# An attention layer on one core: three turns of the probabilities moved ahead of two chunks of the output projection

## The reference

```python
xn = layernorm(x)                                  # x: (4, 512, 1024)
q, k, v = xn @ Wq.T, xn @ Wk.T, xn @ Wv.T          # 32 query heads, 8 key/value heads, 128 wide
q, k = rmsnorm(q) * q_norm_w, rmsnorm(k) * k_norm_w
scores = q @ k.T / sqrt(128) + alibi_bias          # causal
out = softmax(scores) @ v
s = concat_heads(out) @ Wo.T
g = silu(xn @ W.T + bias + lora(xn))
y = x + s * g
```

## Time and profile before

| what | value |
|---|---|
| median of 3 runs | 2855.52 us (2854.84 to 2856.85) |
| the profiled execution: its own time | 2851.0 us |
| the profiled execution: its span, first to last instruction | 2849.2 us |
| PE busy | 2763.9 us, 97% of the span |
| DVE, ACT, POOL busy | 2198.6 us (77%), 1259.9 us (44%), 1136.4 us (40%) |
| mean granted TensorE clock | 0.990 of full speed |

### The profile page before, as it was taken

How to read it: one execution, slowest core, us unless ns; L and a number is a source line. 1 busy time by engine, 2 the same in 40 slices (tenths; PEclk the granted TensorE clock), 3 DMA queues, 4 the chain that set the end, 5 groups by cost and what they waited for, 6 DMA issues and landing times.

```text
span 2849.2 us, 47788 instructions
## 1 busy us (share of the span) xinstructions
PE 2763.9 (97%) x18256; PEld 2516.4 (88%) x18256; DVE 2198.6 (77%) x5317; ACT 1259.9 (44%) x2907; POOL 1136.4 (40%) x555
## 2 busy tenths in 40 slices
PE   7999999998999999999899999999989999999997
PEld 6899999997889999999688999999878999999985
DVE  6877777778787777777878777777787877777788
ACT  3444444444344444444434444444443444444443
POOL 3334334333434434334353334443344433344334
PEclk9999999999999999999999999999999999999999
DMA  7222222212422221221341222222224222222213
GB/s 256 97 79 67 65 70 64 64 61 96 168 66 86 75 67 60 68 75 57 106 168 52 72 75 75 67 69 65 71 96 160 67 61 66 75 75 68 74 62 113
DMA packets 80659, 240.40 MB, mean 84 GB/s; under 512 B 9008, under 2 KB 17328, under 8 KB 79920
## 3 DMA queue, kind: packets, MB, share of 16 engines
q1 hardware_dynamic: 80432, 237.35, 25.2%
HBM read 217.39 MB, written 19.92 MB: 83 GB/s over the span
## 4 chain that ended last, share of the span: by engine, by line
PE 83%; DVE 14%; issue 2%; ACT 0%; DMA 0%; SPq 0%; POOL 0%; POOLq 0%; DVEq 0%; ACTq 0%
PE proj L402 20%; PE proj L403 20%; PE proj L404 20%; PE tr L472 4%; PE sc L402 3%; PE ot L403 3%; PE ot L404 3%; PE sc L404 3%; PE sc L403 3%; DVE g_buf L1155 3%; PE ot L402 3%; PE tr L484 2%; DVE sq L1060 2%; DVE prob L1126 1%; DVE xtok L1050 1%
## 5 line engine op out<-in xcount | busy, mean ns | idle before, releaser
L916 POOL TENSOR_TENSOR wb_lo<-stage_b,wb_hi 128x1024 fp32r<-128x1024 f32 x158 | 382.3, 2419 | 1424.6 <-ACT wb_hi L684 1424.6
L402 PE MATMUL proj<-wa_hi,xn_hi 128*128 128x256 f32 x3072 | 878.3, 286 | 0.9 <-issue 0.9
L404 PE MATMUL proj<-wa_hi,xn_lo 128*128 128x256 f32 x3072 | 869.3, 283 | 0.0
L403 PE MATMUL proj<-wa_lo,xn_hi 128*128 128x256 f32 x3072 | 869.2, 283 | 0.0
L402 PEld LDWEIGHTS proj<-wa_hi,xn_hi 128*128 128x128 f32 x3072 | 589.0, 192 | 2.5 <-issue 2.1
L403 PEld LDWEIGHTS proj<-wa_lo,xn_hi 128*128 128x128 f32 x3072 | 589.3, 192 | 0.3
L404 PEld LDWEIGHTS proj<-wa_hi,xn_lo 128*128 128x128 f32 x3072 | 588.9, 192 | 0.0
L911 POOL TENSOR_TENSOR wa_lo<-stage_a,wa_hi 128x1024 fp32r<-128x1024 f32 x192 | 463.1, 2433 | 228.7 <-ACT wa_hi L670 228.7
L709 ACT ACTIVATE prob<-prob,negmax 128x128 f32<-128x128 f32 (+3 forms) x512 | 286.5, 560 | 431.0 <-DVE negmax L1116 430.1
L402 PE MATMUL proj<-o_hi,wb_hi 128*128 128x512 f32 x1024 | 431.5, 421 | 41.7 <-DVE acc L1143 40.3
L1143 DVE TENSOR_TENSOR acc<-acc,proj 128x512 f32<-128x512 f32 x480 | 326.9, 682 | 116.0 <-PE proj L404 113.3
(11 more groups left out here) (120 smaller groups left out, 4778.9 us busy)
## 6 DMA issues: line engine op xcount, KB each, us to landing
stage_a<-wa SPq DMA_DIRECT2D x196, 512.0 KB, 3.6
stage_b<-wo SPq DMA_DIRECT2D x128, 512.0 KB, 3.7
stage_b<-weff SPq DMA_DIRECT2D x30, 512.0 KB, 3.8
xtok<-x_tok SPq DMA_DIRECT2D x4, 2048.0 KB, 8.6
outT<-acc SPq DMA_DIRECT2D x32, 256.0 KB, 2.0
gate_dram<-x_buf SPq DMA_DIRECT2D x28, 256.0 KB, 2.2
xtok<-xT SPq DMA_DIRECT2D x16, 256.0 KB, 4.1
xtok<-gate_dram SPq DMA_DIRECT2D x16, 256.0 KB, 4.7
```

Of the source, the lines that this page charges most:

```text
L402: pe.matmul(out, hi_l, hi_r, start=first, stop=False)
L403: pe.matmul(out, hi_l, lo_r, start=False, stop=False)
L404: return pe.matmul(out, lo_l, hi_r, start=False, stop=last)
L916: pool.tensor_tensor(wb_lo[:, slot, :], stage_b[:, slot, :], wb_hi[:, slot, :], ALU.subtract).then_inc(wb_ready, 1)
```

## The change

In the middle groups (`early`), PE does the turns of the key tiles 0 to 2 straight behind the projections, ahead of chunks 0 and 1. The order becomes: turns 0 to 2, chunks 0, 1, 2, (the turn of the queries in j = 3,) the turn of tile 3, chunk 3. PE's wait for the normalised probabilities (`prob_ready`) moves up with them. DVE's order follows: the low parts of tiles 0 to 2 stand behind the row statistics and ahead of the addition of chunk 0. In j = 3 the addition of chunk 1 stands straight behind the scaling of the rows. ACT's, POOL's and SP's programs are as they were, and so is every instruction's work.

```diff
@@ PE, body @@
+                    early = not first and not last
+                    c = 23 if last and j == 3 else 5 * j + 1
+                    if early:
+                        pe.wait_ge(prob_ready, pos.at(4, j + 1))
+                        turn_probs(pos, c, (0, 1, 2))
                     if not late_gate:
                         pe.wait_ge(wb_ready, pieces + SLOT2)
                         pe.wait_ge(ot_free, pos.at(4, 3 if j >= 2 else 1))
                         out_proj(pos, j, pair, slot, (0, 1))
-                    pe.wait_ge(prob_ready, pos.at(4, j + 1))
-                    c = 23 if last and j == 3 else 5 * j + 1
-                    turn_probs(pos, c, (0, 1, 2))
+                    if not early:
+                        pe.wait_ge(prob_ready, pos.at(4, j + 1))
+                        turn_probs(pos, c, (0, 1, 2))
@@ DVE, body @@
+                    early = not first and not last
+                    c = 23 if last and j == 3 else 5 * j + 1
+
+                    def prob_lo(k, c):
+                        w = slice(PT_AT[k], PT_AT[k] + S - P * k)
+                        take_lo(pos, c + k, pT_lo[:, w], pT_hi[:, w], slice(P * k, S))
+
+                    if early:
+                        for k in range(3):
+                            prob_lo(k, c)
                     if adds:
                         add_out(pos, j, 0, half, first)
                     if ended is not None:
                         row_factors(pos, ended)
                     if j == 3 and ended is not None:
                         scale_rows(ended)
+                        if early:
+                            add_out(pos, j, 1, half + 1, first)
                     elif adds:
                         add_out(pos, j, 1, half + 1, first)
-                    c = 23 if last and j == 3 else 5 * j + 1
                     for k in range(NT):
                         if k == 3:
...
-                        w = slice(PT_AT[k], PT_AT[k] + S - P * k)
-                        take_lo(pos, c + k, pT_lo[:, w], pT_hi[:, w], slice(P * k, S))
-                        if k == 1 and j == 3 and ended is not None:
+                        if k == 3 or not early:
+                            prob_lo(k, c)
+                        if k == 1 and j == 3 and ended is not None and not early:
                             add_out(pos, j, 1, half + 1, first)
```

## The result

The changed kernel takes **3004.05 us** (median of 4 runs, 3002.08 to 3007.02) against 2855.91 us for the kernel before (median of 4, 2854.84 to 2856.85): ratio 1.052, 95% interval 1.0501 to 1.0538. It is 148 us slower. The forecast was 3022 us, in a range of 2960 to 3070.

A forecast was written before the change was run, and what follows sets the result against it. PE was taken as the bound, busy 97% of the span. Waits of 150 us in 24 middle groups plus 17 us of clock falls, on the 2855.5 us median, gave 3022 us, range 2960 to 3070.

The forecast's parts named there:

- The exchange on PE: Middle groups: nine transposes ahead of twelve matmuls on PE, in either order 3.66 us until chunk 2 can start; no loss.
- DVE's order, chunk 2: Middle groups: chunk 2 waits for chunk 0's addition, behind three low parts; 1.84, 1.5, 0 and 1.2 us lost by stage.
- The collision: j = 3 of middle groups: DVE's small steps and scaling run inside POOL's subtraction; chunk 3 1.1 to 2.9 us late in all.
- The high end: j = 3: all DVE steps held until POOL's subtraction ends at 321.0, chunk 3 at 322.95, 2.9 us lost in all.
- two held rows: Kernel before, under POOL subtractions: a scaling took 2.13 us instead of 0.69, a small step 1.77 us.
- rival of a smaller collision: j = 3: DVE's steps pass POOL's subtraction or POOL starts later, no clock fall; 107 us lost, 2963 us, chance 0.2.
- The sum: Middle groups: 1.84 + 1.5 + 0 + 2.9 = 6.2 us each, times 24 = 150 us.
- The clock: j = 3 of middle groups: a fall to half clock in half of the groups, 1.4 us each, 17 us.
- rival of more falls: Clock falls at each wait near 2 us, in j = 0 and j = 3 of all 24 groups; 3073 us, chance 0.22.
- The fast side: j = 3: earlier turns free banks, chunk 3's 0.28 us hold-up goes; 6.7 us gained, 2849 us, chance 0.03.

The follow-up runs named there:

- j = 2 alone: The change made only in the stages j = 2 of the middle groups of the kernel before: 2856.54 us against 2855.01, ratio 1.0006.
- the hold-up of j = 3: Kernel before with DVE's addition of chunk 1 straight behind the scaling in j = 3 of groups 0 to 6: 2856.74 us, ratio 1.0001.
- a new order there: On top of the hold-up of j = 3, two of group 7's four scalings moved behind additions of chunks 1 and 2: 2830.18 us against 2855.01.

## Why the prediction was right, and where it was off

**The exchange on PE.** It was costed at nothing, and so was the wait for the probabilities. In j = 2, where nothing else is late, turns and three chunks take 0.90 + 4.21 = 5.11 us, and before they took 3.66 and 1.46 for chunk 2, as long; none of the new waits is for the probabilities. PE's order alone costs 37 us beside DVE's old order, so it is free only if DVE frees the turns' banks as early as the change does, and there the additions pay for it.

**DVE's order, chunk 2.** Late by 1.84, 1.5, 0 and 1.2 us was forecast for the four stages; 1.70, 1.48, 0 and 1.10 us came, and in j = 2 the addition had 0.40 us to spare where 0.3 was forecast. One length was misread: the 0.6 us from the first high part to the first low part isn't in the rows named, where it is 262.92 - 262.09 = 0.83 us with DVE still at an addition; in the changed kernel it is 270.60 - 269.99 = 0.61 us, so the sum lost nothing by it. The causes were tried. With the two weight pieces out of the way the loss of j = 1 goes; with the square roots out of the way as well the lateness of chunk 2 shrinks to 0.60 us in j = 0 and goes in j = 3.

**The collision.** The high end, 2.9 us for j = 3, was taken because of two held rows; 2.84 us came, and the step was held to within 0.02 us of POOL's end. With POOL's subtraction moved away, the wait went. This also fells the rival of a smaller collision (2963 us). The Trainium skill (SBUF — State Buffer, SBUF: two separate sides) says that a VectorE operation with two SBUF inputs and a GpSimd operation that reads SBUF exclude each other for the whole instruction. The 2.06 us here agree with it; the 0.16 us beside the bias do not. DVE's low parts, which read one input from PSUM, were not held: under the moved subtraction (321.09 to 323.50) three of them took 1.49 us as before.

**The sum.** Without the clock it was 150 us; 148 were measured, 146 of them in the 24 middle groups. In the list of waits I had put the additions at 150 us; 124.8 came, because idle time shows less than lateness (1.44 for 1.70), with the same 72 new waits.

**The clock** is the term that failed: "I expect one in half of the groups, in j = 3", 17 us. No fall came in any middle stretch: the granted clock there is 1.00 behind waits of 1.44, 1.23, 0.86 and 1.65 us. The forecast of 3022 was 18 us high, 17 of them by this term. The step behind it was to take the wait of 2.00 us as a neighbour of waits up to 1.9 us; the run with DVE's order alone shows falls behind most of its waits of 2.26 us, so falls behind waits of this kind are real, but none of the change's waits brought one. The rival of more falls (3073 us) fell with it.

**The fast side.** The rival named 24 x 0.28 = 6.7 us. Taking just that hold-up away gave 2856.74 against 2855.01 us: no such gain was there to be had, as the next stage takes most of it back.

## What to carry to other kernels

An engine that runs its instructions in order pays for an early step with everything queued behind it: before moving a step up, look at who waits for what stands behind it, and at the chain that the step itself waits for. Where the engine that sets the time has no idle time in the stretch, as PE here, a new order has next to nothing to gain: the two orders tried there that cost nothing (j = 2 alone, and the hold-up of j = 3) gained at most 0.1 us a group. The search belongs to the places where that engine does wait: a new order there gave 0.9%. Put the operation that the bounding engine waits for ahead of those that nobody waits for yet.

## What the runs showed of the hardware that was not expected

Waits of PE that the timeline shows as 0.86 to 1.65 us idle, four in a group of 84.8 us, left the granted clock at 1.00. With equal waits of 2.26 us it fell to half in 65 of 96 stages and stayed up in the others, and one and the same stage, j = 2, shows both. In the kernel before, 2.00 us brought a fall and 2.63 didn't. So neither the length of the last wait nor its place in the group decides alone; what does is open.

A hold on DVE depended on what POOL ran: 0.16 us for a small step beside POOL's bias (a product with a scalar), 2.06 us beside its subtraction of two tensors. In the kernel before all 24 such first steps beside the bias took 0.16 us. One case goes the other way: in group 7 of each batch a step that started 0.07 us after the bias (672.24 and 672.17) took 0.63 us; why is open. In the kernel before, the four scalings of group 7 took 7.22 us in all, the shortest 0.80 and the longest 2.86, the last two of them under POOL's subtractions. A part of what that edit won may be that the scalings meet these less; that was not measured apart.
